# A fused attention and expert layer: the first stage's input loaded turned and normalised by GpSimd, with the keys' pieces joined and set half a slot earlier

## The reference

```python
def layernorm(x, eps=1e-05):
    return (x - mean(x)) / sqrt(var(x) + eps)
def attention(x):            # Wq, Wk, Wv, Wo: 256 x 256
    q, k, v = (heads(x @ W.T) for W in (Wq, Wk, Wv))
    score = where(causal, q @ k.T / 4, -inf)
    return merge(softmax(score) @ v) @ Wo.T
def experts(h):              # router, then 2 of 8 experts a row
    w, at = top_k(softmax(h @ router.T + bias), 2)
    gate = minimum(gate(h), 7); up = clip(up(h), -7, 7)
    return sum over 2 of w * down((up + 1) * gate * sigmoid(1.702 * gate))
x = x + layernorm(attention(layernorm(x)))
x = x + layernorm(experts(layernorm(x)))
```

## Time and profile before

| what | value |
|---|---|
| median of 3 runs | 1973.91 us (1972.45 to 1975.69) |
| the profiled execution | 1974.26 us, span 1972.6 us |
| TensorE busy | 1843.6 us, 93% of the span |
| VectorE busy | 1545.3 us, 78% |
| ScalarE busy | 1316.8 us, 67% |
| GpSimd busy | 863.7 us, 44% |
| granted TensorE clock, mean | 0.979 |
| DMA | 411.85 MB, mean 209 GB/s |

### The profile page before, as it was taken

How to read it: one execution, slowest core, us unless ns; L and a number is a source line. 1 busy time by engine, 2 the same in 40 slices (tenths; PEclk the granted TensorE clock), 3 DMA queues, 4 the chain that set the end, 5 groups by cost and what they waited for, 6 DMA issues and landing times.

```text
span 1972.6 us, 77603 instructions
## 1 busy us (share of the span) xinstructions
PE 1843.6 (93%) x27790; PEld 1325.9 (67%) x27791; DVE 1545.3 (78%) x5221; ACT 1316.8 (67%) x3291; POOL 863.7 (44%) x1247
## 2 busy tenths in 40 slices
PE   6899999999999999999999899999999999999980
PEld 3255555555555555555554469899999999999970
DVE  3888888888888888888898648778777777777767
ACT  4277788878888888888788765554444545554437
POOL 4323343445546455455454734544333333333336
PEclk9799999999999999999999999999999999999995
DMA  6734656565555646455558569889899999998858
GB/s 199 223 120 128 196 172 206 163 203 180 177 176 165 196 141 199 147 177 181 153 167 246 166 207 271 240 253 259 260 259 264 258 262 263 266 261 245 239 120 341
DMA packets 255070, 411.85 MB, mean 209 GB/s; under 512 B 34480, under 2 KB 191920, under 8 KB 247600
## 3 DMA queue, kind: packets, MB, share of 16 engines
q1 hardware_dynamic: 217856, 363.46, 57.5%
q0 software_dynamic: 27120, 35.40, 10.2%
q10 hardware_dynamic: 9792, 8.93, 1.5%
HBM read 284.83 MB, written 122.28 MB: 206 GB/s over the span
## 4 chain that ended last, share of the span: by engine, by line
PE 82%; DVE 8%; ACT 4%; issue 4%; DMA 2%; SPq 1%; POOL 0%; DVEq 0%; ACTq 0%; POOLq 0%
PE ps_s L1525 18%; PE ps_s L1351 11%; PE ps_w L1351 11%; PE ps_o L1404 10%; PE ps_e L1351 10%; PE ps_e L1525 6%; PE ps_e L1542 6%; PE ps_o L1542 6%; DVE cmax L769 2%; ACT arena L1143 2%; PE ps_e L1535 1%; DVE space L128 1%; DVE arena L766 1%; DVE space L790 1%; PE ps_w L1485 1%
## 5 line engine op out<-in xcount | busy, mean ns | idle before, releaser
L1143 ACT ACTIVATE arena<-ps_e 128x512 f32<-128x512 f32 (+3 forms) x1536 | 688.6, 500 | 190.6 <-PE ps_e L1351 174.9
L766 DVE CUSTOM_DVE_ANT_0 arena<-ps_s,c 128x384 bf16<-128x384 f32 (+3 forms) x1024 | 462.8, 485 | 101.6 <-PE ps_s L1351 93.4
L1351 PE MATMUL ps_s<-arena 96*32 96x512 bf16 (+3 forms) x6144 | 518.1, 333 | 15.0 <-DVE rmax L766 6.8
L1351 PE MATMUL ps_e<-arena 98*32 98x512 bf16 (+3 forms) x6144 | 510.5, 327 | 10.3 <-ACT arena L1143 9.1
L769 DVE TENSOR_REDUCE cmax<-ps_s 128x1 f32<-128x512 f32 x512 | 322.0, 679 | 42.0 <-PE ps_s L1351 41.3
L1404 PE MATMUL ps_o<-arena 128*32 128x256 f32 (+3 forms) x4096 | 344.9, 407 | 2.5 <-POOL arena L663 2.3
L1351 PEld LDWEIGHTS ps_s<-arena 96*32 96x32 bf16 x6144 | 175.9, 96 | 189.7 <-DVE rmax L766 60.6
L1351 PEld LDWEIGHTS ps_e<-arena 98*32 98x32 bf16 x6144 | 179.6, 97 | 149.8 <-issue 36.2
L646 POOL DMA_INDIRECT acc<-blank,place_now x135 | 212.9, 1577 | 147.0 <-DMA acc<-blank,place_now 76.1
L1525 PE MATMUL ps_s<-arena 128*128 128x128 f32 x2192 | 268.7, 276 | 0.0
L663 POOL TENSOR_SCALAR_AFFINE_SELECT arena<-arena 128x512 f32<-128x512 f32 x256 | 162.8, 636 | 239.2 <-ACT arena L1143 238.5
(11 more groups left out here) (182 smaller groups left out, 2720.1 us busy)
## 6 DMA issues: line engine op xcount, KB each, us to landing
arena<-in_gate_up SPq DMA_DIRECT2D x91, 1024.0 KB
arena<-qk_parts SPq DMA_DIRECT2D x384, 128.0 KB
c_h<-in_gate_up SPq DMA_DIRECT2D x44, 1024.0 KB
qk_parts<-space SPq DMA_DIRECT2D x120, 192.0 KB
d_xin<-xs SPq DMA_DIRECT2D x136, 130.5 KB, 3.3
arena<-v_aug SPq DMA_DIRECT2D x32, 512.0 KB, 5.2
o_t<-ot SPq DMA_DIRECT2D x64, 256.0 KB
v_aug<-space SPq DMA_DIRECT2D x28, 512.0 KB, 5.7
```

The source lines that it names most:

```text
L766: dve.tensor_tensor_reduce(summed[:, m % RJ, 0:w], ps_s[:, m % RS, 0:w], after[:, HALF - w:HALF], 1.0, LOWEST, ALU.add, ALU.max, rmax[:, p ...
L1143: act.activation(pw[:, n % RP, 0:w], ps_e[:, n % RE, 0:w], ACT.Exp, scale=SCALE).then_inc(e_done, 1)
L1351: last = pe.matmul(out[at:at + QUAD], lhsT[:, at:at + QUAD], rhs, start=start, stop=stop)
```

## The change

For the pairs from 6 on, x is no longer normalised and then turned. The host passes x turned as well (`x_turned`, 256 x 8192). SP loads the pair's turned tile straight into `xn_t`. The two statistics of a row (1/root and shift) are turned into rows by one small matmul against the identity (`turn_norms`), copied out by ScalarE, stored to DRAM by SP and read back spread over all 128 partitions. GpSimd multiplies the turned tile by the first row and adds the second. Queries and keys start a slot earlier (`Q_AT` = `A_AT` - 1); the keys' four steps come in two pieces instead of three, the first in the third step of a slot, the second after the first step of the next. The first part and the remainder of the keys move a step forward in their slots. The routing moves from step 1 to step 3 of its slot. The pairs 0 to 5 keep their old way, but for the joined pieces. Two semaphores of GpSimd's statistics are joined into one, in stages A and C, so that the root waits for both operations ahead of it.

```diff
+    Q_AT = [start if a < FIRST_EVEN else start - 1 for a, start in enumerate(A_AT)]
+    NORM_AT = [start - (12 if a == FIRST_EVEN else 13) for a, start in enumerate(A_AT)]
+        norm_rows = space[:, 2560:3072].rearrange("p (z t) -> p z t", z=2)
+        a_norm = sb("a_norm", [P, 2, 2, 2])
+        a_rstd, a_shift = a_norm[:, :, 0], a_norm[:, :, 1]
+        norm_row = sb("norm_row", [4, P])
+        turned_v = x_turned.rearrange("(k p) (a t) -> a p k t", p=P, t=WIDE)
+        norms_v = norms.rearrange("a z (c p) -> a (z c) p", p=P)
...
 # SP
-                        sp.wait_ge(a_xn, a - 1 if a < EARLY else a + 1)
+                        if a < FIRST_EVEN:
+                            sp.wait_ge(a_xn, a - 1 if a < EARLY else a + 1)
+                        else:
+                            sp.wait_ge(a_st, a + 1)
                         sp.dma_start(ax[:, a % 2], x_v[a + 2]).then_inc(ax_in[a % 2], 16)
+                for a in due(A_AT, -12, g):
+                    if a >= FIRST_EVEN:
+                        sp.wait_ge(norms_sb, a - FIRST_EVEN + 1)
+                        sp.dma_start(norms_v[a], norm_row[:]).then_inc(norms_out, 16)
+                for a in due(A_AT, -10, g):
+                    if a >= FIRST_EVEN:
+                        u = a % 2
+                        sp.wait_ge(a_v, a - 1)
+                        sp.wait_ge(a_xt, a)
+                        sp.dma_start(xn_t[:, u], turned_v[a]).then_inc(turned_in, 16)
+                        sp.wait_ge(norms_out, (a - FIRST_EVEN) * 16 + 16)
+                        if a == FIRST_EVEN:
+                            sp.wait_ge(a_tps, FIRST_EVEN)
+                        sp.dma_start(norm_rows, norms[a:a + 1].broadcast_to([P, 2, WIDE])).then_inc(turned_in, 16)
...
 # GpSimd
-                for u, (at, done_by, n) in enumerate(((BEGIN - 2, a_p3, 2 * EARLY + 2), (BEGIN + 6, a_p3, 2 * EARLY + 4), (BEGIN + 9, a_p3, 2 * EARLY + 4))):
+                for u, (at, done_by, n) in enumerate(((BEGIN - 2, a_p3, 2 * EARLY + 2), (BEGIN + 6, a_p3, 2 * EARLY + 4), (BEGIN + 9, a_xt, FIRST_EVEN + 1))):
...
-                    pool.tensor_tensor(a_var[:, u], a_mv[:, u, :, 1], consts["eps"][:, 0:2], ALU.add).then_inc(a_varred, 1)
-                    pool.tensor_tensor(a_minus[:, u], a_mv[:, u, :, 0], consts["minus"][:, 0:2], ALU.mult).then_inc(a_negated, 1)
-                    pool.wait_ge(a_varred, a + 1)
+                    pool.tensor_tensor(a_var[:, u], a_mv[:, u, :, 1], consts["eps"][:, 0:2], ALU.add).then_inc(a_moved, 1)
+                    pool.tensor_tensor(a_minus[:, u], a_mv[:, u, :, 0], consts["minus"][:, 0:2], ALU.mult).then_inc(a_moved, 1)
+                    pool.wait_ge(a_moved, 2 * a + 2)
                     pool.tensor_tensor(a_rstd[:, u], a_var[:, u], consts["power"][:, 0:2], ALU.pow).then_inc(a_rooted, 1)
-                    pool.wait_ge(a_negated, a + 1)
                     pool.wait_ge(a_rooted, a + 1)
                     pool.tensor_tensor(a_shift[:, u], a_minus[:, u], a_rstd[:, u], ALU.mult).then_inc(a_shifted, 1)
+                for a in due(A_AT, -7, g):
+                    if a >= FIRST_EVEN:
+                        u, mine = a % 2, xn_t[:, a % 2]
+                        pool.wait_ge(turned_in, (a - FIRST_EVEN) * 32 + 32)
+                        pool.tensor_tensor(mine, mine, norm_rows[:, 0:1].broadcast_to([P, KT, WIDE]), ALU.mult).then_inc(a_scaled, 1)
+                        pool.wait_ge(a_scaled, a - FIRST_EVEN + 1)
+                        pool.tensor_tensor(mine, mine, norm_rows[:, 1:2].broadcast_to([P, KT, WIDE]), ALU.add).then_inc(a_xt, 1)
...
-                for a in due(A_AT, 6, g):
+                for a in due(Q_AT, 6, g):
                     third(a, 1)
-                for a in due(A_AT, 3, g):
+                for a in due(Q_AT, 3, g):
                     third(a, 0)
...
 # VectorE: remainder(a, 1) from step 3 to step 2
                     if s == 2:
+                        for a in due(Q_AT, 4, g):
+                            remainder(a, 1)
...
-                        for a in due(A_AT, 2, g):
+                        for a in due(Q_AT, 2, g):
                             remainder(a, 0)
-                        for a in due(A_AT, 4, g):
-                            remainder(a, 1)
...
 # ScalarE
+                    if s == 1:
+                        for a in due(NORM_AT, 0, g):
+                            if a >= FIRST_EVEN:
+                                act.wait_ge(norms_ps, a - FIRST_EVEN + 1)
+                                if a > FIRST_EVEN:
+                                    act.wait_ge(norms_out, (a - FIRST_EVEN) * 16)
+                                act.activation(norm_row[:], ps_w[0:4, 0:P], ACT.Copy).then_inc(norms_sb, 1)
...
+                    if s == 1:
+                        for a in due(Q_AT, 4, g):
+                            first_part(a, 1)
                     if s == 2:
-                        for a in due(A_AT, 0, g):
+                        for a in due(A_AT[0:FIRST_EVEN], 0, g):
...
-                        for a in pairs_due(-2, -10, g):
+                        for a in due(A_AT[0:FIRST_EVEN], -2, g):
...
 # TensorE
+            def turn_norms(a):
+
+                bank_free()
+                used.append((norms_sb, a - FIRST_EVEN + 1))
+                pe.wait_ge(a_shifted, a + 1)
+                pe.matmul(ps_w[0:4, 0:P], a_norm[:, a % 2].rearrange("p z c -> p (z c)"), consts["ident"],
+                          start=True, stop=True).then_inc(norms_ps, 1)
...
                     if s == 0:
-                        for a in due(A_AT, 4, g):
-                            q_or_k(a, 1, (1,))
+                        for a in due(NORM_AT, 0, g):
+                            if a >= FIRST_EVEN:
+                                turn_norms(a)
+                        for a in due(Q_AT, 4, g):
+                            q_or_k(a, 1, (2, 3))
                     if s == 1:
-                        for a in due(A_AT, 0, g):
+                        for a in due(A_AT[0:FIRST_EVEN], 0, g):
                             turn_over(a)
-                        for a in due(A_AT, 1, g):
+                        for a in due(Q_AT, 1, g):
                             q_or_k(a, 0, (0, 1))
-                        for a in due(A_AT, 2, g):
+                        for a in due(Q_AT, 2, g):
                             q_or_k(a, 0, (2, 3))
-                        for a in due(A_AT, 4, g):
-                            q_or_k(a, 1, (2, 3))
...
                     if s == 2:
-                        for a in due(A_AT, 3, g):
-                            q_or_k(a, 1, (0,))
+                        for a in due(Q_AT, 3, g):
+                            q_or_k(a, 1, (0, 1))
...
+                    if s == 3:
                         for r in rows_due(16, 17, 17, g):
                             route(r, 0)
                             route(r, 1)
```

More of the change, by code:

```diff
@@ L1583, in _ @@
                             turn_rows(r)
+                        for n in groups_due(NEVER, 23, g, 1):
+                            rank(n)
+                    if s == 2:
+                        for a in due(Q_AT, 3, g):
+                            q_or_k(a, 1, (0, 1))
+                        if 0 < g <= NE * QUADS and apart_of(g - 1) == 2:
+                            weigh(g - 1, 0, 2)
+                    if s == 3:
                         for r in rows_due(16, 17, 17, g):
```

54 lines of the change are left out of this document (21 added, 33 removed).

## The result

| | before | after |
|---|---|---|
| median of 4 executions, us | 1974.30 (1972.45 to 1975.69) | 2017.86 (2016.42 to 2022.49) |
| profiled execution / its span, us | 1974.26 / 1972.6 | 2016.42 / 2014.7 |
| first exponential starts, us | 95.6 | 108.1 |
| from there to the start of the last one | 1055.3 | 1083.1 |
| from there to the end of the span | 821.7 | 823.5 |

The ratio is 1.0226, with a 95% interval of 1.0209 to 1.0243. Of the 42.2 us between the two profiled executions 12.5 lie ahead of the first exponential, 27.8 in the attention part and 1.8 behind it. The forecast had 19.6, 22 and 0.

The account below looks back on a forecast made before the run. The prediction took TensorE (busy 93%) as the bound, coupled to VectorE and ScalarE by rings of banks. It summed 1974.3 + 22 (quads) + 19.6 (start) = 2016 us, range 1987 to 2036.

Parts of the forecast that it names:

- the routing's wait, -0.12: Slot 7: the routing's wait on the logits before the transposes was counted as gone, -0.12 us a quad.
- The old waits, -0.44 and -0.99: Two TensorE waits were to go: a score waiting for ScalarE's burst (0.44 us), the values' matmuls waiting for VectorE's remainder (0.99).
- a_shift, +0.88: Slot 7: the new small matmul makes TensorE wait for GpSimd's a_shift, +0.88 us a quad, bounds 0.6 and 1.0.
- Slot 10, +1.10: Slot 10: a score waits for ScalarE, where c_y follows the queries' first part; +1.10 us, bounds 0.5 and 1.2.
- Slots 11 to 2: TensorE needs 9.2 us, but waits on VectorE's load bring the total to 10.44: +1.2, bounds 0 and 2.
- The ranking quads, +0.2: The four quads where the second stage's ranking runs have no wait for a_shift: +0.2 us each.
- GpSimd, 0, with a margin of 0.1: Slot 1's two new operations cost nothing: statistics end at 13.2, ScalarE wants them at 13.3; upper bound 1 us.
- The start, +19.6: Before the first quad: TensorE goes on 17.8 us later, -1.7 regained, +0.5 a_shift, +3 low clock; between 12 and 24.
- The first (1922): Whole kernel: TensorE's saved work and three old waits count, no new wait comes, start hidden; -52 us, 1922; chance 0.08.
- The second (a hidden start, 1996): Steady quads as forecast, but the start hidden because SP is earlier or loads land sooner; 1996 us; chance 0.12.
- The third, that waits pay for each other: Start as forecast, but VectorE and ScalarE catch up in the new waits and quads keep their length; 1994 us; chance 0.2.
- The fourth: GpSimd late in slots 1 to 3, ScalarE waits for the statistics: 1 us more in 20 quads, 2036; chance 0.12.

Follow-up runs that it names:

- e4: Changed kernel with the turned input alone: queries' and keys' pieces, first part, remainder and routing at the steps of the kernel before; 1991.0 us (1.0076).
- e5: Kernel before with only the keys' pieces joined, and the remainder at step 2 of slot 0; 1964.39 us (0.9943).
- e2: Changed kernel with the small matmul of the norms and ScalarE's copy at step 2 of their slot, for pairs 7 to 31; 2001.44 us (1.0138).
- e6: Kernel before with the routing's matmuls at step 3 of slot 7 instead of step 1; 1980.33 us (1.0018).
- e12: Kernel before with the routing at step 3 and the two semaphores of each statistic joined into one; 1980.8 us (1.003).
- e3: Changed kernel with ScalarE's second-stage normalisation c_y at step 1 of slot 9, ahead of the queries' first part; 2014.38 us (1.0201).
- e10: Changed kernel with one line undone: queries' and keys' work of pairs 6 to 31 starts in its old slot; 1980.98 us (1.0036).
- e7: Changed kernel with the edits of e1, e2 and e3, and VectorE's comparison for the ranking a slot later; 1991.67 us (1.0071).
- e9: Changed kernel with two more GpSimd additions of zero on the turned 128x512 tile in slot 1; 2048.87 us (1.0378).
- e11: e10 with e1's edit, the ranking's comparison in slot 2, the small matmul at slot 8, step 1, and the routing at step 1 of slot 7; 1948.75 us (0.9873).
- e1: Changed kernel with the first turned pair's multiply and add on GpSimd moved behind the last memset and the row of maxima; 2009.2 us (1.0169).

## Why the prediction was right, and where its terms were off

- **The transposes, -0.70, and the routing's wait, -0.12.** The first is right: slot 8 without the transposes is 0.71 shorter (e4). Of the second nothing is left in it.
- **The old waits, -0.44 and -0.99.** The first is right: slot 11 is 0.43 shorter in e4. Of the second slot 1 shows 0.73, of which the joining alone brings 0.33 (e5).
- **a_shift, +0.88.** The place and the releaser are right: slot 7 is 1.00 longer with the matmul's own 0.16, and the rows show 0.65 idle. But part of slot 7's growth belongs to the routing. The wait itself is worth 0.60 (e2), the routing's new step 0.17 to 0.20 (e6), which the forecast counted as a gain of 0.12. The two errors cancel. The joined semaphore delays the root by 0.12 (e12), where the forecast had 0.17; how much of it TensorE waits is not shown.
- **Slot 10, +1.10.** Measured 1.07. c_y is only 0.31 of it (e3); without c_y the keys' wait for the remainder comes out. "The keys' own wait for the remainder (0.5) ends inside it" was the half that mattered more.
- **Slots 11 to 2.** Forecast 10.44 against 11.51, measured 10.35; of it slots 11 and 0 were to take 5.68, measured 5.46.
- **The ordinary quad, 34.9.** 34.89 to 34.90. Quads 0 to 3, without c_y: 32.9 against 32.3, forecast +0.65. The forecast kept TensorE's work and counted waits; e10 gives the loss by slots, 0.86 and 1.07 against 0.40, and puts 1.55, more than the whole +1.1, on the half slot forward.
- **The ranking quads, +0.2.** Measured +1.27: the term that was most mis-sized. The +0.2 is an ordinary quad's +1.1 without the wait for a_shift; it has no term for the ranking's comparisons on VectorE, which now stand beside GpSimd's multiply and take 1.33 instead of 0.22. Four quads, 4.3 us above the forecast.
- **Late quads, 0.** Measured +0.33 in the two plain ones, of it 0.20 the routing; 0.13 is open. Quads 25 to 30 together come out even.
- **GpSimd, 0, with a margin of 0.1.** Right for ordinary quads, where the margin was 1.47 by the trace, and wrong for the ranking ones, as said.
- **The start, +19.6.** Measured +12.5. The chain is right; SP's arrival at the turned load was 4.4 us too late in the forecast, and the clock's +3 was nothing.
- **One quad** of 36.18 came on top, 1.28 us (a late issue on GpSimd, below). The kernel before has one like it, 35.12 instead of 33.80: there TensorE sat idle for 1.99 in slot 1, with no releaser named. Here is that row. The two cancel.

```profile
436.19 0.28 PE L1351 MATMUL ps_s<-arena 96*32 96x256 bf16 x1 [1.99 <-issue]
```

By quads, counted from slot 0, the first four cost +2.8 (forecast 2.6), the sixteen ordinary ones +16.9 (17.6), the four ranking ones +5.1 (0.8) and the next +0.7 (0.65). Another 2.3 lies in the last quad and at the two ends of the attention part (0). So +19.6 that should have been 12.5, and +22 that should have been 27.8, made 2016 against 2017.86. The length of an ordinary quad came out right, though several of its terms are off. That the total fits to 2 us, with the start some 7 us too high and the rest as much too low, is luck.

**The rivals.** The first (1922) needed no new wait: both its conditions failed. The second (a hidden start, 1996) failed, though the start is smaller. The third, that waits pay for each other, is refuted by e2 and e7, where what is taken from one slot comes off the quad whole. The fourth is false at the kernel's load and true at twice that load (e9).

## What to carry to other kernels

Before a step is moved, ask of the slot that receives it whether TensorE has room there, and of the one that loses it whether TensorE was what made it long; here 0.86 went into a full slot and nothing came out of slot 0. When an engine off the path gets a new operation, look at what the other engines run beside it: VectorE's short operations can be held for the length of GpSimd's. And when a queue runs behind its plan at the start, an instruction with a far-off due date can stand ahead of the one that everything waits for: move the first instance alone.

## What the runs showed of the hardware that was not expected

**VectorE held by GpSimd.** A VectorE comparison of two arrays took 0.22 us alone and 1.33 beside GpSimd's 128x512 multiply; a cast of 128x16 took 0.17 in one kernel and 1.27 to 1.29 in e3, five times in a row. The reductions from ps_s kept their times. The Trainium skill ("SBUF — State Buffer", section "SBUF: two separate sides") describes an exclusive port pair shared by the two, taken by whichever starts first for its whole instruction. The trace agrees: in e3 GpSimd began 0.03 us ahead, and VectorE ended 0.04 us behind it. The page names VectorE operations with two SBUF inputs, as the comparison is, and those in a two-port mode; whether the cast and the operation on 128x8 ran in such a mode no run here shows.

**A late issue on GpSimd, once.** In each of the fourteen kernels GpSimd issues the DMA of the maxima's rows 0.30 us behind VectorE's copy, but the 21st time 1.58 behind it, 1.28 late. Of the others from the second on only the last is off by more than 0.02 (0.44). Timelines of GpSimd, before and then after:

```profile
760.52 0.79 POOL L672 DMA_DIRECT2D arena<-mrow  x1 [2.61 <-issue]
```

```profile
790.50 0.79 POOL L693 DMA_DIRECT2D arena<-mrow  x1 [2.61 <-issue]
...
825.40 0.78 POOL L693 DMA_DIRECT2D arena<-mrow  x1 [1.33 <-DVE mrow L809]
```

Before, that quad took 33.80 like its neighbours. After, it took 36.18 instead of 34.90, for TensorE now hangs on GpSimd's chain without slack: its wait for a_norm was 1.94 there. In e11, where the small matmul stands a slot later, slots 7 and 8 of that quad are 2.97 and 2.30, as in any other: the late issue costs nothing. What GpSimd does in that time no row says.

**The clock fell in the middle of the stream.** In e1, e4 and e10 slot 7 of that quad is 6.8 to 6.9 us long, not 5.25. TensorE's timeline and the view by stretches of e10:

```profile
768.80 0.27 PE L1464 MATMUL ps_w<-c,a_norm 128*4 128x128 f32 x1 [1.95 <-POOL a_norm L706]
```

```profile
769.00:772.40 3.40, 3.40 (x40) 1.74 (x33) 1.50 (x3) 1.34 (x3) 1.85 (x2) 0.50 0.36 122
```

The granted clock was 0.50 (1.2 GHz) from 769.0 to 772.4, behind that wait, and the scores took 1.02 instead of 0.43. In the three kernels it cost 1.6 to 1.7 us on top of the 1.28. In the changed kernel TensorE waited 1.94 at the same place and kept 1.00; what decides it is open.
